# State-space layer: the sum over states by accumulating transposes, a quarter of the inputs on ScalarE, gate and gated result on GpSimd

## The reference, cut to what matters

```python
xn = _layernorm(x, ln_gamma, ln_beta)
proj = xn @ W_in + b_in
u, res = jnp.split(proj, 2, axis=-1)
u = silu(causal 4-tap convolution of u)
dt, Bm, Cm = jnp.split(u @ W_x, [64, 80], axis=-1)
delta = softplus(dt @ W_dt + b_dt)
# for each of 16 states n: h_n[t] = exp(delta*A_n) * h_n[t-1] + delta*u*B_n[t]
# y[t] = sum over n of h_n[t] * C_n[t]
y = (y + u * D) * silu(res)
return y @ W_out + b_out + x
```

## Time and profile before

| what | value |
|---|---|
| time, median of 3 runs | 2707.77 us (2706.87 to 2712.53) |
| the profiled execution, its own time | 2685.25 us |
| its span, first to last instruction | 2683.4 us |
| PE busy over the span | 2112.3 us (79%) |
| DVE busy | 1731.5 us (65%) |
| ACT busy | 1330.2 us (50%) |
| POOL busy | 1261.9 us (47%) |
| granted TensorE clock, mean | 0.872 of full speed |
| scans of the layer, first and last start | 1770.3 us and 2362.1 us |

### The profile page before, as it was taken

One profiled execution on the slowest core, in us unless ns is written; L12 is line 12 of the kernel. 1 busy time (PEld: TensorE's weight loads), 2 busy tenths in 40 slices (PEclk: granted clock), 3 DMA queues, 4 the chain that ended last, 5 costly groups with the idle time before them and its releaser, 6 DMA issues. The chain is left out here.

```text
span 2683.4 us, 47828 instructions
## 1 busy us (share of the span) xinstructions
PE 2112.3 (79%) x15968; PEld 1469.5 (55%) x15968; DVE 1731.5 (65%) x4210; ACT 1330.2 (50%) x2849; POOL 1261.9 (47%) x1313
## 2 busy tenths in 40 slices
PE   5899999899986793196599996679999999852770
PEld 3566666666675583074255555656655566541550
DVE  5777777776757573012677764758888888857213
ACT  5565656565432373032255554556666666630223
POOL 5645554554311005444321114567877778720672
PEclk8999999999996595598599997889999999965895
DMA  8300000000020000122333340000000000010113
GB/s 235 84 1 2 1 2 2 2 1 2 2 71 0 0 0 29 58 65 77 94 90 77 93 119 1 0 1 1 0 0 0 0 0 0 0 32 0 41 53 96
DMA packets 104252, 89.45 MB, mean 33 GB/s; under 512 B 12076, under 2 KB 91206, under 8 KB 104006
## 3 DMA queue, kind: packets, MB, share of 16 engines
q1 hardware_dynamic: 96934, 72.67, 10.1%
q0 software_dynamic: 7168, 14.73, 1.8%
HBM read 59.02 MB, written 40.96 MB: 37 GB/s over the span
## 5 line engine op out<-in xcount | busy, mean ns | idle before, releaser
L3340 POOL TENSOR_SCALAR mb_w<-mb_duT,mb_bT 128x256 f32<-128x256 f32 x512 | 466.8, 931 | 122.8 <-PE bank L3350 61.3
L3275 DVE TENSOR_TENSOR_SCAN mb_hs<-mb_dA,bank 128x512 f32<-128x512 f32 x256 | 300.7, 1204 | 38.8 <-issue 24.6
L3369 PE MATMUL bank<-mb_hc,ident 128*128 128x512 f32 x512 | 263.2, 639 | 12.4 <-DVE mb_hc L3285 11.7
L38 POOL TENSOR_TENSOR scrap<-ones 128x1 f32<-128x1 f32 x64 | 12.4, 193 | 517.3 <-DVE gla_ss L412 309.3
L3331 ACT ACTIVATE mb_dA<-mb_delta,mb_A 128x255 f32<-128x255 f32 x512 | 216.6, 495 | 9.2 <-DVE mb_hs L3275 9.0
L2497 DVE TENSOR_REDUCE ra_mx<-bank 128x2 f32<-128x512 f32 x256 | 163.7, 685 | 59.4 <-PE bank L2351 56.8
L2079 ACT ACTIVATE e_hid<-bank,e_b 128x512 f32<-128x512 f32 (+1 forms) x128 | 81.1, 634 | 235.0 <-PE bank L2123 232.1
L2587 ACT ACTIVATE ra_pT<-bank 128x512 f32<-128x512 f32 x256 | 141.1, 600 | 112.5 <-PE bank L2373 112.4
L563 DVE TENSOR_TENSOR gla_mid<-bank,gla_ex 128x512 f32<-128x512 f32 x128 | 88.0, 688 | 149.0 <-ACT gla_ex L549 149.0
L3350 PE MATMUL bank<-ident,mb_w 128*128 128x128 f32 x1024 | 151.9, 283 | 34.3 <-DVE mb_hs L3275 26.2
L579 DVE COPY_PREDICATED gla_sT<-c_seen,bank 128x768 f32<-128x768 int32 x128 | 130.6, 1020 | 37.5 <-issue 37.5
(11 more groups left out here) (536 smaller groups left out, 5720.8 us busy)
## 6 DMA issues: line engine op xcount, KB each, us to landing
results<-const_empty SPq DMA_DIRECT2D x2, 4096.0 KB
e_got<-results SPq DMA_DIRECT2D x32, 256.0 KB, 3.3
rope_rows<-ra_part SPq DMA_DIRECT2D x48, 128.0 KB, 1.9
ra_k<-rope_rows SPq DMA_DIRECT2D x32, 192.0 KB, 3.4
ra_q<-rope_rows SPq DMA_DIRECT2D x32, 192.0 KB, 4.4
queue<-const_spare_rows SPq DMA_DIRECT2D x1, 4128.0 KB
e_x<-queue SPq DMA_DIRECT2D x8, 516.0 KB, 4.2
e_w<-in_L_ffn_w SPq DMA_DIRECT2D x2, 2048.0 KB, 8.8
```

What stands on the lines that cost most here:

```text
L3275: dve.tensor_tensor_scan(hs[n // 2 % 2][:, n % 2, :, :].rearrange("p c t -> p (c t)"), dA[n % RD][:, :, :].rearrange("p c t -> p (c t)"), ...
L3340: ins = pool.tensor_scalar(w[n % RH][:, h, :], duT[k][:, h, :], bT[k][:, h, n:n + 1], None, ALU.mult)
L3369: ins = pe.matmul(YB[:, :], g.ident[:, :], hc[grp % 2][:, j, :, :].rearrange("p c t -> p (c t)"), start=(n == 0), stop=(n == NS - 1))
```

## The change

The sum over states becomes transposes that accumulate in PSUM: the product block is the stationary operand, the identity the moving one, and YB then holds y with tokens on the partitions. ScalarE copies YB to SBUF (`act_result`, at its step 1 of the next body), TensorE transposes it back into channels in bank RB (`pe_channels`, step 2), and `dve_finish` moves to step 3 and only adds u*D. GpSimd makes the gate in two instructions (`pool_gate`) and multiplies by it (`pool_finish`). The inputs w of states 3, 7, 11 and 15 are made by ScalarE (`act_inputs`, three steps before the state) and the other twelve by GpSimd. `pe_out` moves from step 4 to step 6, behind that step's sum, `dve_residual` from 7 to 9, and TensorE's stage 9 from step 9 to 10. In the diff, context is left out.

```diff
...
+    yT = g.xT[:, 0:2 * DI].rearrange("p (h d) -> p h d", h=2)
...
-             "st", "mv", "mvs"]
+             "st", "mv", "mvs", "yT", "yb", "wa", "yg", "gp"]
-     st_ready, mv_ready, mvs_ready) = [sig(n) for n in names]
+     st_ready, mv_ready, mvs_ready, yT_ready, yb_psum, wa_ready, yg_ready, gp_ready) = [sig(n) for n in names]
...
-    def dve_gate(dve, s, k):
-        dve.wait_ge(er_ready, s + 1)
-        dve.scalar_tensor_tensor(out=gr[k][:, :, :], in0=e2[:, :, :], scalar=1.0, in1=rs[:, :, :],
-                                 op0=ALU.add, op1=ALU.mult).then_inc(gr_ready, 1)
     def dve_finish(dve, s, k):
-        dve.wait_ge(y_psum, s * (NS // 2) + NS // 2)
+        dve.wait_ge(yb_psum, s + 1)
-                                           in1=YB[:, c * 256:(c + 1) * 256], op0=ALU.mult, op1=ALU.add)
+                                           in1=RB[:, c * 256:(c + 1) * 256], op0=ALU.mult, op1=ALU.add)
-        dve.wait_ge(yy_ready, s * 2 + 1)
-        dve.wait_ge(gr_ready, s + 1)
-        dve.tensor_tensor(yy[k][:, :, :], yy[k][:, :, :], gr[k][:, :, :], ALU.mult).then_inc(yy_ready, 1)
     def dve_residual(dve, s):
...
+    def by_act(n):
+        return n % RH == RH - 1
+    PER_POOL, PER_ACT = NS - NS // RH, NS // RH
     def pool_inputs(pool, s, k, n):
...
+    def act_inputs(act, s, k, n):
+        act.wait_ge(duT_ready, s + 1)
+        if n >= RH or not first(s):
+            act.wait_ge(dbu_psum, s * NS + (n - RH + 1))
+        for h in range(2):
+            ins = act.activation(w[n % RH][:, h, :], duT[k][:, h, :], ACT.Copy, scale=bT[k][:, h, n:n + 1])
+        ins.then_inc(wa_ready, 1)
+    def pool_gate(pool, s, k):
+        pool.wait_ge(er_ready, s + 1)
+        if s >= 2:
+            pool.wait_ge(yg_ready, s - 1)
+        pool.tensor_tensor(gr[k][:, :, :], e2[:, :, :], rs[:, :, :], ALU.mult).then_inc(gp_ready, 1)
+        pool.wait_ge(gp_ready, s + 1)
+        pool.tensor_tensor(gr[k][:, :, :], gr[k][:, :, :], rs[:, :, :], ALU.add).then_inc(gr_ready, 1)
+    def pool_finish(pool, s, k):
+        pool.wait_ge(yy_ready, s + 1)
+        pool.wait_ge(gr_ready, s + 1)
+        pool.tensor_tensor(yy[k][:, :, :], yy[k][:, :, :], gr[k][:, :, :], ALU.mult).then_inc(yg_ready, 1)
     def pe_inputs(pe, s, n):
-        pe.wait_ge(w_ready, s * NS + (n + 1))
+        if by_act(n):
+            pe.wait_ge(wa_ready, s * PER_ACT + (n // RH + 1))
+        else:
+            pe.wait_ge(w_ready, s * PER_POOL + (n - n // RH + 1))
...
     def pe_sum(pe, s, grp):
         pe.wait_ge(hc_ready, s * (NS // 2) + (grp + 1))
         if grp == 0 and not first(s):
-            pe.wait_ge(yy_ready, s * 2 - 1)
+            pe.wait_ge(yT_ready, s)
         for j in range(2):
             n = 2 * grp + j
-            ins = pe.matmul(YB[:, :], g.ident[:, :], hc[grp % 2][:, j, :, :].rearrange("p c t -> p (c t)"),
-                            start=(n == 0), stop=(n == NS - 1))
+            for h in range(2):
+                for c in range(ND):
+                    at = h * DI + c * P
+                    ins = pe.matmul(YB[:, at:at + P], hc[grp % 2][:, j, c, h * P:(h + 1) * P], g.ident[:, :],
+                                    start=(n == 0 and at == 0), stop=(n == NS - 1 and at == 3 * P), is_transpose=True)
         ins.then_inc(y_psum, 1)
-    def pe_out(pe, s, k):
-        pe.wait_ge(yy_ready, s * 2 + 2)
+    def pe_channels(pe, s):
+
+        pe.wait_ge(yT_ready, s + 1)
         if not (isinstance(s, int) and s == NSEQ - 1):
             pe.wait_ge(r_ready, s + 2)
+        for c in range(ND):
+            for h in range(2):
+                ins = pe.transpose(RB[:, c * SEQ + h * P:c * SEQ + (h + 1) * P], yT[:, h, c * P:(c + 1) * P], g.ident[:, :])
+        ins.then_inc(yb_psum, 1)
+
+    def act_result(act, s):
+        act.wait_ge(y_psum, s * (NS // 2) + NS // 2)
+        if not first(s):
+            act.wait_ge(yb_psum, s)
+        act.activation(yT[:, :, :], YB[:, :].rearrange("p (h d) -> p h d", h=2), ACT.Copy).then_inc(yT_ready, 1)
+
+    def pe_out(pe, s, k):
+        pe.wait_ge(yg_ready, s + 1)
         for h in range(2):
             o = RB[:, h * P:(h + 1) * P]
             for c in range(ND):
...
-    PE_WHEN = {0: (0,), 1: (1,), 2: (2,), 6: (4,), 7: (5,), 8: (7,), 9: (9,), 11: (6,)}
-    IN_PLACE, FINISH, OUT, RESIDUAL, GATE = 0, 2, 4, 7, 7
+    PE_WHEN = {0: (0,), 1: (1,), 2: (2,), 6: (4,), 7: (5,), 8: (7,), 10: (9,), 11: (6,)}
+    IN_PLACE, BACK, FINISH, POOL_GATE, POOL_FINISH, OUT, RESIDUAL = 0, 2, 3, 4, 7, 6, 9
     def turns(start, body, end):
...
-            if n == GATE and nxt is not None:
-                dve_gate(dve, s, k)
...
     def dve_end(dve):
-        dve_gate(dve, NSEQ - 1, 1)
...
+            if n == 1 and not first(s):
+                act_result(act, s - 1)
+            if n % RH == 0:
+                act_inputs(act, s, k, n + RH - 1)
     def act_end(act):
+        act_result(act, NSEQ - 1)
     def pe_start(pe):
...
+            if n == BACK and not first(s):
+                pe_channels(pe, s - 1)
...
     def pe_end(pe):
+        pe_channels(pe, NSEQ - 1)
     def nothing(eng):
...
-                    pool_inputs(pool, s, s % 2, n)
+                    if not by_act(n):
+                        pool_inputs(pool, s, s % 2, n)
+                    if n == POOL_GATE:
+                        pool_gate(pool, s, s % 2)
+                    if n == POOL_FINISH and s:
+                        pool_finish(pool, s - 1, 1 - s % 2)
+            pool_finish(pool, NSEQ - 1, 1)
         def _(dve):
...
```

## The result

| what | before | after |
|---|---|---|
| median of the timed runs | 2706.8 us (6 runs, 2698.46 to 2712.53) | 2718.57 us (6 runs, 2715.41 to 2724.97) |
| ratio after : before, 95% interval | | 1.005 (1.0029 to 1.007) |
| span of the profiled execution | 2683.4 us | 2715.8 us |
| first to last delta of the layer, 15 periods | 560.9 us | 569.0 us |

The account below looks back on a forecast made before the run. Bound: the order of waits between nearly full TensorE and VectorE. Delta-to-delta terms sum to 38.9 us against 37.4: 1.5 for each of 14 sequences, +21, with the ends +17; on 2707.77 that gives 2725 us, range 2700 to 2788.

Parts of the forecast that it names:

- The three waits: On VectorE: before u*D 3.1 us for the channel transposes, before u 3.45 for the projection, before delta about 0.8.
- The sum by transposes: On TensorE, eight accumulating 128x128 transposes replace four 512-column instructions: 1.04 us a group, where each sum held it 1.73.
- TensorE's share: TensorE's busy share of the layer would fall from 93% to near 70%.
- ScalarE's gap: ScalarE idled 2.66 us before xT; two input pairs (1.64) and the YB copy (0.60) would fill nearly all of it.
- That cover: GpSimd's multiplication, 1.3 us, fits some 6 us between VectorE's steps 3 and 6, so it is just covered.
- The base of the comparison: The period of the kernel before, 37.4 us; the forecast 38.9 adds 1.5 for each of 14 sequences, +21.
- The slow stretch: TensorE at 1.2 GHz in the stretch following 2058.6 to 2062.0 us, expected to stay as short and mostly off the cycle.
- The ends: First body -2 us, last body about -2.5, tail +0.5, beside +21 for the 14 sequences between.
- A: Transposes don't raise TensorE's clock, which stays slow: 42.5 us per sequence, +67, 2775 us; chance 0.20.
- D: Accumulating transposes on TensorE cost as matmuls: 1.4 us more per sum on the cycle, 41.7, 2764 us; chance 0.05.
- B: At VectorE's step 3 the wait for the channels vanishes: cycle 35.8 us, -26, 2682 us; chance 0.13.
- C: B in part: ScalarE's pairs overlap better or the projection's wait is shorter; +0 to +3, 2707 to 2711; chance 0.12.

Follow-up runs that it names:

- the mended order: Changed kernel with the transposes back moved from step 2 to step 1 and the projection from step 6 to step 4: 2662.16 us, ratio 0.984.

## Why the prediction was right

It said slower, 2725 us; 2718.57 was measured, inside the range. Point by point, the terms of the cycle:

| term | predicted | measured |
|---|---|---|
| delta to duT | 3.80 | 3.74 (2066.53 to 2070.27) |
| ScalarE to the convolution's start | 10.98 | 10.70 (to 2080.97) |
| TensorE to u*D | 4.43 | 4.18 (to 2085.15) |
| VectorE, u*D to the sum of group 2 | 6.61 | 6.52 (to 2091.67) |
| sum, broadcast, projection | 3.45 | 3.34 (to 2095.01) |
| u to delta | 9.65 | 9.65 (to 2104.66) |
| sum | 38.9 | 38.13 |

- *The three waits* were named in place and releaser. Before u*D 3.1 forecast and 2.42 found, before u 3.45 and 3.40, before delta 0.8 and 0.72. In all 7.3 forecast and 6.5 found. The prediction set this against 3.5 before the change; with the 0.68 that it overlooked it was 4.2, in the periods at 37.55 that it took its rows from.
- *The sum by transposes* was taken at 1.04 us with the last one's drain included (the row cited has 1.07). On the cycle it is 0.87 to 0.93 from start to start, since the broadcast behind it starts while it drains. That, and the same overlap in the transposes back (0.64 with hand-over for 0.73) and in ScalarE's list, make the 0.8 us by which the sum was too long. Whole durations of the rows had been added where starts follow each other sooner.
- *TensorE's share* was forecast near 70% and is 77%. This was a slip against my own terms: 93% of 37.4 is 34.9, less 5.5 and plus 0.45 is 29.9, and of 38.9 that is 77%.
- *ScalarE's gap* before xT vanished, as said. GpSimd's multiplication (1.27 us) comes 0.1 after u*D and is done long before the projection, as said. That cover was real and thin: the run with all inputs on GpSimd shows it gone.
- *The base of the comparison* was 37.4 a period. The second profile of the kernel before has 37.1 on average, so the loss per period is 1.1 (38.2 less 37.1), for 1.5 forecast. At full clock on both sides it is 1.4 (38.13 less 36.77).
- *The slow stretch* was said to lie mostly off the cycle. That holds for the changed kernel, but not for the kernel before, where a period with it is 0.8 longer.
- *The ends.* The first period came out at 34.32, 2.9 below the second profile's 37.23, for a gain of 2 forecast. From the last delta to the layer's end I had a gain of 2.0 and found a loss of about 0.7 (52.5 us against 51.8). The body up to the tail did gain 3, and the tail lost nearly 4: VectorE waits 3.86 us for the transposes back and 5.26 for the projection, where it waited 1.48 for the sum and 3.12 for the projection. About half of that is the clock, by an estimate from the rows that follow. It is low from before the last sum on:

```profile
2374.30:2384.60 10.30, 6.80 (x24) 5.13 (x24) 1.32 (x3) 1.36 (x3) 1.26 (x1) 0.50 0.00 0
```

  In the run with the projection back at step 4 it is 1.00 there (2338.80 to 2343.40), and from the last sum to the projection takes 4.74 us and not 6.07. The projection itself took 3.86 us to the residual where it took 3.07 before, with half of its matmuls still at full clock then. For the rest, I had counted bare instructions without the hand-overs between the engines, and subtracted a gate that lay beside the wait for the sum.
- Together: 14 periods at 1.1 make 15, less 2.9 and plus 0.7 is 13, against 12 measured and 17 forecast. The nearness is in part luck: the cycle was too long by 0.7 a period and the base by 0.3, and the two ends were off by 1 and 3 us in opposite directions.

**The rivals.** A, the slow clock, is refuted: over 2033 to 2071 the granted clock is 1.00, where it was 0.96, and over the last 14 periods it is 0.98, as in the second profile of the kernel before. D, transposes at the price of matmuls, is refuted by the 0.87. B, faster, needed the way back 3.1 us earlier than my chain; it is what the mended order gives, not the changed one. C lay 8 us lower than the result.

What the prediction did not see is how the loss divides. It named the moves of the way back and of the projection as what decides, and did not say that these two constants hide a gain of 43 us against the kernel before. The experiments put values on the parts, each taken in the mended order: the transposes 41 us, ScalarE's inputs 27, gate and multiplication on GpSimd nothing, or 10 once the inputs of state 11 are moved. The values don't add up, as each is bounded by the next wait. Why the periods with all inputs on GpSimd alternate between 35.2 and 36.6 isn't known, and no slot was tried for ScalarE's copy of YB other than ahead of xT.

## What to carry to other kernels

When one engine's work is made cheaper in a kernel with a hand-written order, lay out the cycle again and look at what stands in that engine's queue in front of each result that another engine waits for: here two constants outweighed three changes of real work. A wait that is removed is worth the distance to the next late operand, not its own length, so two fixes have to be tried together before either is judged (the way back's slot brought 13 us alone and 17 on top of the projection's), and two delays of the same hand-over hide each other until both are gone.

## What was not expected of the hardware

**Transposes alone brought the full clock back.** In the mended kernel TensorE sits idle 2.06 us and soon after runs at half clock. Its timeline:

```profile
2214.43 0.90 PE L3373 MATMUL bank<-ident,mb_w 128*128 128x128 f32 x4 [2.06 <-DVE mb_hs L3276]
2215.13 1.06 PE L3267 MATMUL bank<-ident,mb_z 128*128 128x128 f32 x4
2215.98 1.06 PE L3373 MATMUL bank<-ident,mb_w 128*128 128x128 f32 x4
2216.83 1.69 PE L3395 MATMUL bank<-ident,mb_hc 128*128 128x128 f32 x8
2218.36 0.38 PE L3382 MATMUL bank<-mb_bc,mb_sel 128*128 128x256 bf16 x2
...
2219.94 1.09 PE L3373 MATMUL bank<-ident,mb_w 128*128 128x128 f32 x8 [1.20 <-ACT mb_w L3346]
```

and the granted clock over that stretch and the next (windows view):

```profile
2214.75:2218.05 3.30, 3.30 (x18) 3.13 (x16) 3.30 (x5) 1.86 (x5) 1.14 (x2) 0.50 0.00 0
2218.20:2221.50 3.30, 2.10 (x19) 1.82 (x18) 2.81 (x3) 3.30 (x10) 3.30 (x5) 1.00 0.00 0
```

From 2214.43 to 2218.36 TensorE runs nothing but fp32 transposes. At 1.2 GHz four take 1.06 us, and from the last of them on the clock is 2.4 GHz and eight take 1.09. The same happens from 2121.00 to 2125.12 in the run with the projection back at step 4. So the clock rose while transposes alone ran, which the prediction had found shown by no row. The Trainium skill, "TensorE: Matmul & The Clock Gate", Part 4, says that the full clock doesn't engage for the transpose mode, as it doesn't count as PE-busy in the same way; this stretch is against it for fp32, and the measurement decides. Why the start of the layer stayed at the lower level, with transposes alone and TensorE busy 4.59 of 6.8 us, no run shows.

**VectorE and GpSimd in each other's way.** The multiplication of two operands took VectorE 0.87 to 1.01 us in both profiles of the kernel before, beside a GpSimd that was at work, and 0.69 in the last sequence, where GpSimd was done. Back on VectorE in the mended order it takes 0.69 in all 16 sequences, but then GpSimd's two instructions that begin 0.28 us after it take 2.11 us, where a pair takes 1.82 with no such neighbour (four take 3.63). First GpSimd's instruction beside the multiplication of the earlier trace rows (t = 73.34), then the gate and the multiplication on VectorE in the mended order, each with what GpSimd started beside it:

```profile
2073.33 0.93 POOL L3340 TENSOR_SCALAR mb_w<-mb_duT,mb_bT 128x256 f32<-128x256 f32 x1
```

```profile
2031.86 0.67 DVE L3292 SCALAR_TENSOR_TENSOR mb_gr<-mb_e,mb_rs 128x512 f32<-128x512 f32 x1
2032.03 1.29 POOL L3346 TENSOR_SCALAR mb_w<-mb_duT,mb_bT 128x256 f32<-128x256 f32 x1
...
2057.36 0.69 DVE L3303 TENSOR_TENSOR mb_uc<-mb_uc,mb_gr 128x512 f32<-128x512 f32 x1
2057.64 2.11 POOL L3346 TENSOR_SCALAR mb_w<-mb_duT,mb_bT 128x256 f32<-128x256 f32 x2 [2.00 <-PE bank L3381]
```

The overlap costs 0.3 to 0.4 us (the single instruction beside the gate takes 1.29, for 0.91 otherwise). In these three cases the instruction that started second was the longer one (in the first by a lead of only 0.01 us); no run varies the order on purpose. The Trainium skill, "Perfetto Trace Analysis", section "Optimizing Scalar/DVE Operations", says that the two engines share a read port, which some VectorE operations hold alone; the trace agrees in these operations.
